# A transformer program on one core: new order in the ternary stage, three weight places in the expert stage, gathers ahead of a barrier

## The reference

```python
# block 0, feed-forward ("ffn0")
def act_quant(x):
    scale = 127.0 / jnp.clip(jnp.max(jnp.abs(x), axis=-1, keepdims=True), 1e-05)
    return jnp.clip(jnp.round(x * scale), -128, 127) / scale
h = bit_linear(x, w1)            # ternary weights, 256 -> 1024, input by act_quant
h = depthwise_conv1d(h.transpose(0, 2, 1), conv_w, conv_b)   # 3 taps over the positions
h = jax.nn.silu(h.transpose(0, 2, 1))
return bit_linear(h, w2)         # 1024 -> 256, input by act_quant

# block 1, feed-forward: 8 experts, 2 for each token ("moe"), then a layer norm ("norm2")
topv, topi = jax.lax.top_k(probs, K)
for e in range(E):
    h = jax.nn.relu(tok @ w1[e].T + b1[e]) @ w2[e].T + b2[e]
    moe_out = moe_out + combine[:, e:e + 1] * h
return _ln(x + moe_out, ln2_g, ln2_b)
```

## Time and profile before

| | us |
|---|---|
| median of 3 runs (lowest, highest) | 1503.93 (1497.29, 1506.65) |
| profiled execution, its own time | 1496.67 |
| its span, first to last instruction | 1495.1 |
| TensorE busy, share of the span | 76% |
| VectorE busy | 57% |
| GpSimd busy | 32% |
| ScalarE busy | 26% |
| TensorE's granted clock, mean (1 is 2.4 GHz, 0.5 is 1.2 GHz) | 0.856 |

### The profile page before, as it was taken

One profiled execution on the slowest core, in us unless ns is written; L12 is line 12 of the kernel. 1 busy time (PEld: TensorE's weight loads), 2 busy tenths in 40 slices (PEclk: granted clock), 3 DMA queues, 4 the chain that ended last, 5 costly groups with the idle time before them and its releaser, 6 DMA issues.

```text
span 1495.1 us, 20996 instructions
## 1 busy us (share of the span) xinstructions
PE 1141.2 (76%) x7256; PEld 951.7 (64%) x7257; DVE 855.3 (57%) x1924; ACT 381.6 (26%) x799; POOL 479.4 (32%) x351
## 2 busy tenths in 40 slices
PE   6889488884688696999469989999734998924574
PEld 4778376663577554898368878888623876612343
DVE  3676677855576547888512222222176785367985
ACT  1445122221455311111012212222211443201111
POOL 3434312234466023567640110000272332102210
PEclk9889699996799897999779999999865999555856
DMA  8998000000000200000341322110130000000000
GB/s 286 397 387 301 1 1 2 17 1 0 1 1 1 79 2 0 1 12 33 126 172 50 147 87 81 35 35 32 42 107 0 2 1 1 0 0 1 15 21 21
DMA packets 42860, 93.49 MB, mean 63 GB/s; under 512 B 3821, under 2 KB 16654, under 8 KB 39974
## 3 DMA queue, kind: packets, MB, share of 16 engines
q1 hardware_dynamic: 35254, 62.24, 11.5%
q0 software_dynamic: 7536, 30.32, 5.7%
HBM read 39.02 MB, written 51.51 MB: 61 GB/s over the span
## 4 chain that ended last, share of the span: by engine, by line
PE 60%; DVE 20%; issue 7%; POOL 5%; ACT 4%; DMA 3%; POOLq 1%; DVEq 0%; SPq 0%; ACTq 0%
PE PS L1864 9%; PE PS L1854 9%; PE PS L802 7%; PE PS L1131 3%; PE PS L785 3%; PE PS L815 3%; PE PS L1391 3%; PE PS L1731 3%; PE PS L775 2%; PE PS L757 2%; POOL big L1991 2%; PE PS L684 1%; PE PS L1720 1%; PE PS L2521 1%; PE PS L754 1%
## 5 line engine op out<-in xcount | busy, mean ns | idle before, releaser
L1854 PE MATMUL PS<-scr 128*128 128x128 f32 x1184 | 147.7, 285 | 14.1 <-DMA scr<-ew_in 9.6
L1854 PEld LDWEIGHTS PS<-scr 128*128 128x128 f32 x1184 | 146.1, 201 | 18.0 <-issue 13.4
L1864 PE MATMUL PS<-scr 128*128 128x256 f32 x592 | 136.6, 384 | 11.2 <-PE PS L1840 11.2
L1864 PEld LDWEIGHTS PS<-scr 128*128 128x128 f32 x592 | 109.6, 190 | 32.1 <-issue 18.9
L554 POOL TENSOR_TENSOR scr<-scr,big 128x1232 f32<-128x1232 f32 x32 | 72.0, 2249 | 142.5 <-DVE big L404 142.5
L1900 DVE TENSOR_SCALAR scr<-PS,W 128x128 f32<-128x128 f32 x148 | 51.5, 351 | 114.2 <-PE PS L1854 114.2
L1886 ACT ACTIVATE scr<-PS,W 128x128 f32<-128x128 f32 x148 | 54.3, 367 | 232.3 <-PE PS L1854 232.3
L1928 POOL DMA_DIRECT2D expert_out<-scr x37 | 20.1, 544 | 260.6 <-DVE scr L1906 260.6
L1906 DVE TENSOR_TENSOR scr<-PS,W 128x256 f32<-128x256 f32 x37 | 15.7, 425 | 146.0 <-PE PS L1864 146.0
L641 ACT ACTIVATE big<-PS 128x512 f32<-128x512 f32 x144 | 74.6, 525 | 96.1 <-PE PS L785 96.0
L785 PE MATMUL PS<-W,scr 128*128 128x128 f32 x480 | 82.8, 296 | 20.8 <-ACT scr L636 8.1
(11 more groups left out here) (382 smaller groups left out, 2364.6 us busy)
## 6 DMA issues: line engine op xcount, KB each, us to landing
expert_in<-zeros SPq DMA_DIRECT2D x1, 19712.0 KB, 60.0
expert_out<-zeros SPq DMA_DIRECT2D x1, 19712.0 KB, 111.9
scr<-ew_in POOLq DMA_DIRECT2D x16, 1024.0 KB, 6.2
scr<-expert_in SPq DMA_DIRECT2D x38, 128.0 KB, 2.0
expert_out<-scr POOLq DMA_DIRECT2D x37, 128.0 KB, 2.0
W<-pack SPq DMA_DIRECT2D x1, 2458.0 KB, 10.0
W<-pack SPq DMA_DIRECT2D x1, 2152.0 KB, 8.2
X<-x_in SPq DMA_DIRECT2D x1, 2048.0 KB, 12.8
```

The costliest lines, as they stand in the source:

```text
L1854: ins = pe.matmul(bank(1 + f % 4, G), e_w1[slot][:, k, f * P:(f + 1) * P], e_xT[:, k, :], start=(k == 0), stop=(k == C - 1))
L1864: ins = pe.matmul(bank(5 + t, D), e_h[:, f, t * P:(t + 1) * P], e_w2[slot][:, f, :], start=(f == 0), stop=(f == FC - 1))
```

## The change

**ffn0.** VectorE takes the statistics ahead of the scales instead of behind them. The maximum is taken apart: its first half stays behind the scales, then come rounding and the evacuation of the hidden products, and only then its second half, the join and the residual. TensorE transposes the maximum (`largest`) in the next turn, between the first two parts of the convolution, makes the output products of sample i-1 between the two halves of the hidden products, and the value or key products (`prepared`) at the end of a turn.

**moe.** The loop over pairs of experts is written out for all eight on every engine. A third weight place lies in `big`, so `slot` is e % 3, and GpSimd loads the weights of expert e + 3 once expert e is stored; those of experts 1 and 2 both at the start. TensorE no longer waits for its own transposes to tell SyncE that the rows' buffer is free; SyncE waits for their signal.

**norm2.** The gathers of samples 0 and 1 are issued at the end of moe, ahead of GpSimd's drain. The gathers are counted by six semaphores: one each for the samples 0, 1, 6 and 7, and one each for the pairs 2, 3 and 4, 5.

Elsewhere, a semaphore of the bias products becomes a count in an existing one, and two memsets share one.

```diff
@@ -943,12 +943,15 @@
                     v.tensor_tensor(f_G[:, 2 * p:2 * p + 2, 1:S + 1], bank(p % 2).rearrange("p (f s) -> p f s", f=2),
                                     f_row1.unsqueeze(1).broadcast_to([P, 2, S]), ALU.mult).then_inc(s["g_ready"], 1)
 
+            def largest_of(i, n):
+
+                v.wait_ge(s["silu_ready"], PAIRS * i + 2 * n + 2)
+                ch.inc(v.tensor_reduce(f_top[:, n, :], f_y[i % 2][:, n * PAIRS:(n + 1) * PAIRS, :].rearrange("p f s -> p s f"),
+                                       AX.X, ALU.max, apply_absolute_value=True))
+
             def largest(i):
 
-                for n in range(2):
-                    v.wait_ge(s["silu_ready"], PAIRS * i + 2 * n + 2)
-                    ch.inc(v.tensor_reduce(f_top[:, n, :], f_y[i % 2][:, n * PAIRS:(n + 1) * PAIRS, :].rearrange("p f s -> p s f"),
-                                           AX.X, ALU.max, apply_absolute_value=True))
+                largest_of(i, 1)
                 ch.sync()
                 v.tensor_tensor(f_amax, f_top[:, 0, :], f_top[:, 1, :], ALU.max).then_inc(s["amax_ready"], 1)
 
@@ -1001,16 +1004,18 @@
             for i in range(B):
                 if i + 1 < B:
                     quantized(i + 1)
+                if i + 2 < B:
+                    stats_of(i + 2)
                 if i:
                     scales(i - 1)
-                if i + 2 < B:
-                    stats_of(i + 2)
+                largest_of(i, 0)
+                if i:
+                    rounded(i - 1)
+                if i + 1 < B:
+                    hidden(i + 1)
                 largest(i)
                 if i:
-                    rounded(i - 1)
                     residual(i - 1)
-                if i + 1 < B:
-                    hidden(i + 1)
                 if i >= 5:
                     key_vars(v, ch, i - 5)
             scales(B - 1)
@@ -1177,6 +1182,8 @@
             pe.wait_ge(s["taps_ready"], FC)
             for i in range(B):
                 convolved(i, 0)
+                if i:
+                    largest(i - 1)
                 convolved(i, 1)
                 if i:
                     row2(i - 1)
@@ -1186,8 +1193,6 @@
                     normed(i + 1)
                     hidden(i + 1, 0)
                     hidden(i + 1, 1)
-                prepared(i)
-                largest(i)
                 if i:
                     if i == 1:
                         pe.wait_ge(s["w_ready"], 2)
@@ -1195,6 +1200,8 @@
                 if i + 1 < B:
                     hidden(i + 1, 2)
                     hidden(i + 1, 3)
+                prepared(i)
+            largest(B - 1)
             row2(B - 1)
             outputs(B - 1)
 
@@ -1250,8 +1257,9 @@
         TABLE_ROWS = -(-(MAX_GROUPS + AHEAD_MAX + 1) // 2) * 2 * G
         xg_dram = nc.dram_tensor("expert_in", (TABLE_ROWS, D), F32, kind="Internal").ap()
         yg_dram = nc.dram_tensor("expert_out", (TABLE_ROWS, D), F32, kind="Internal").ap()
-        e_w1 = [scr[:, n * 4096:n * 4096 + 2048].rearrange("p (c f) -> p c f", c=C) for n in range(2)]
-        e_w2 = [scr[:, n * 4096 + 2048:n * 4096 + 4096].rearrange("p (f d) -> p f d", f=FC) for n in range(2)]
+        e_slot = [scr[:, 0:4096], scr[:, 4096:8192], big[:, 2 * NT * D:2 * NT * D + 4096]]
+        e_w1 = [m[:, 0:2048].rearrange("p (c f) -> p c f", c=C) for m in e_slot]
+        e_w2 = [m[:, 2048:4096].rearrange("p (f d) -> p f d", f=FC) for m in e_slot]
         cut = Cut(scr, 8192)
         e_h = cut(FC * G).rearrange("p (f n) -> p f n", f=FC)
         e_x = scr[:, row8_at:row8_at + GT * D].rearrange("p (t d) -> p t d", t=GT)
@@ -1797,24 +1804,19 @@
 
         def moe_experts(eng, body, row_groups=False):
 
-            with eng.Fori(0, E // 2) as e2:
-                for slot in range(2):
-                    e = 2 * e2 + slot
-                    first = eng.value_load(GROUPS[0:1, bass.ds(e, 1)], min_val=0, max_val=MAX_GROUPS)
-                    last = eng.value_load(GROUPS[0:1, bass.ds(e + E, 1)], min_val=1, max_val=MAX_GROUPS)
-                    ahead = eng.value_load(GROUPS[0:1, bass.ds(e + 2 * E, 1)], min_val=0, max_val=AHEAD_MAX) if row_groups else None
-                    with eng.Fori(first, last) as n:
-                        body(n, slot, ahead if row_groups else e)
+            for e in range(E):
+                first = eng.value_load(GROUPS[0:1, e:e + 1], min_val=0, max_val=MAX_GROUPS)
+                last = eng.value_load(GROUPS[0:1, E + e:E + e + 1], min_val=1, max_val=MAX_GROUPS)
+                ahead = eng.value_load(GROUPS[0:1, 2 * E + e:2 * E + e + 1], min_val=0, max_val=AHEAD_MAX) if row_groups else None
+                with eng.Fori(first, last) as n:
+                    body(n, e % 3, ahead if row_groups else e)
 
         def rows_of(table, n):
             return table[bass.ds(n * G, G), :].rearrange("(t p) d -> p t d", p=P)
 
         def weights_load(eng, e, slot):
-            eng.dma_start(scr[:, slot * 4096:slot * 4096 + 2048], e_w(ew1_in, e)).then_inc(in_expert[slot], 16)
-            eng.dma_start(scr[:, slot * 4096 + 2048:slot * 4096 + 4096], e_w(ew2_in, e)).then_inc(in_expert[slot], 16)
-
-        def e_w(table, e):
-            return table[e] if isinstance(e, int) else table[bass.ds(e, 1), :, :].rearrange("e p n -> p (e n)")
+            eng.dma_start(e_slot[slot][:, 0:2048], ew1_in[e]).then_inc(in_expert[slot], 16)
+            eng.dma_start(e_slot[slot][:, 2048:4096], ew2_in[e]).then_inc(in_expert[slot], 16)
 
         def moe_sp(sp):
             sp.wait_ge(samp["slot_ready"], len(BATCHES) + 1)
@@ -1840,12 +1842,9 @@
                         ins = pe.transpose(bank(0, P, c * G + t * P), e_x[:, t, c * P:(c + 1) * P], ident)
                 ins.then_inc(s["xT_psum"], 1)
 
-                pe.wait_ge(s["xT_psum"], n + 1)
-                pe.sem_inc(s["x_free"], 1)
-
             def body(n, slot, e):
 
-                pe.wait_ge(in_expert[slot], 16 * (e - slot) + 32)
+                pe.wait_ge(in_expert[slot], 32 * (e // 3) + 32)
                 pe.wait_ge(s["xT_ready"], n + 1)
                 for f in range(FC):
 
@@ -1915,26 +1914,36 @@
             vb_zeroed(g, 2)
             g.wait_ge(in_rows, 16)
             weights_load(g, 1, 1)
+            weights_load(g, 2, 2)
             for n in range(2):
                 xs = X[:, n * B:(n + 1) * B, :]
                 g.tensor_tensor(xs, xs, w["ln2b"].unsqueeze(1).broadcast_to([P, B, D]), ALU.add)
 
-            def expert(e, slot):
-                first = g.value_load(GROUPS[0:1, bass.ds(e, 1)], min_val=0, max_val=MAX_GROUPS)
-                last = g.value_load(GROUPS[0:1, bass.ds(e + E, 1)], min_val=1, max_val=MAX_GROUPS)
-                ahead = g.value_load(GROUPS[0:1, bass.ds(e + 2 * E, 1)], min_val=0, max_val=AHEAD_MAX)
+            for e in range(E):
+                first = g.value_load(GROUPS[0:1, e:e + 1], min_val=0, max_val=MAX_GROUPS)
+                last = g.value_load(GROUPS[0:1, E + e:E + e + 1], min_val=1, max_val=MAX_GROUPS)
+                ahead = g.value_load(GROUPS[0:1, 2 * E + e:2 * E + e + 1], min_val=0, max_val=AHEAD_MAX)
                 with g.Fori(first, last) as n:
                     g.wait_ge(s["y_dve"], n + 2)
                     g.dma_start(rows_of(yg_dram, n + ahead), e_y).then_inc(rows_stored, 16)
                     g.wait_ge(rows_stored, 16 * n + 16)
                     g.sem_inc(s["y_sent"], 1)
-
-            with g.Fori(0, E // 2 - 1) as e2:
-                for slot in range(2):
-                    expert(2 * e2 + slot, slot)
-                    weights_load(g, 2 * e2 + slot + 2, slot)
-            for slot in range(2):
-                expert(E - 2 + slot, slot)
+                if e + 3 < E:
+                    weights_load(g, e + 3, e % 3)
+            gathered(g, 0)
+            gathered(g, 1)
+
+        ARRIVALS = [(0,), (1,), (2, 3), (4, 5), (6,), (7,)]
+
+        def arrival_of(i):
+            return [i in group for group in ARRIVALS].index(True)
+
+        def gathered(g, i):
+            for n in range(T * i, T * i + T):
+                for k in range(2):
+                    g.indirect_dma_start(got(k)[:, n, :], None, yg_dram,
+                                         bass.IndirectOffsetOnAxis(ap=SLOT[:, 2 * unit_of(n) + k:2 * unit_of(n) + k + 1], axis=0))\
+                        .then_inc(rows_gathered[arrival_of(i)], 16)
 
         def got(k):
             return e_got[k].rearrange("p (n d) -> p n d", n=NT)
@@ -1945,8 +1954,7 @@
             def summed(i):
 
                 y = n_y[i % 2]
-                if i % 2 == 0:
-                    v.wait_ge(rows_gathered[i // 2], 16 * 4 * T)
+                v.wait_ge(rows_gathered[arrival_of(i)], 16 * 2 * T * len(ARRIVALS[arrival_of(i)]))
                 for k in range(2):
                     for t in range(T):
                         n = T * i + t
@@ -1985,23 +1993,14 @@
         def norm2_pool(g):
             s = norm2
 
-            def gathered(i):
```

(10 more changed lines are left out.)

27 lines of the change are left out of this document (13 added, 14 removed).

## The result

The changed kernel takes 1465.88 us (median of 4 runs, 1462.73 to 1467.81) and the kernel before 1501.6 (4 runs, 1497.29 to 1506.65): a ratio of 0.9757, 95% interval 0.9726 to 0.9788. That is 35.7 us less; I had forecast 21.8 less, taken off a median of 1503.93, and the range ended at 1468. The profiled execution has a span of 1464.5 us, 30.6 less than before.

What follows compares the result with a forecast made beforehand. TensorE was taken to bound moe, a chain across engines ffn0, and GpSimd's queue norm2. Moe -25.9, norm2 -3.0 and ffn0 +7.1 gave -21.8 us off the 1503.93 median: 1482 us, range 1468 to 1494.

Steps and rivals of the forecast that it cites:

- TensorE's wait for its own transposes: In moe, removing this wait saves 0.28 us in each of 37 turns: -10.4 us, between -4 and -11.
- Expert weights: In moe, a third weight place removes two TensorE waits, 4.07 and 5.53 us, and slow products behind: -14.0 us.
- The change of expert: In moe, VectorE's late reading of the next expert's limits, charged 0.6 and 0.8 us where the weight waits go.
- rival C: In moe, the second expert's load delays the next groups' rows, costing 4 us: 1486 us; chance 0.08.
- Loops written out: In moe, dropping the outer expert loop saves 0.2 us at each of seven changes of expert: -1.5 us.
- rival D: In moe, repeated instruction loads cost 2.2 us a turn, making it slower, 1528 us with 21 such turns; chance 0.04.
- The loop of ffn0: The new order's turn takes 21.3 us against 20.44, +0.9, with TensorE waiting 2.8 us in one piece.
- each of four turns pays the lower clock: In ffn0, slow products behind TensorE's longer wait add 1.5 us a turn, from 0 to 3, over four turns.
- The tail: At the end of ffn0, earlier output products and last scales save 2.5 us, 0 to 4.
- the rival (A): TensorE keeps the higher clock in ffn0: 6 us less, 1476 us; chance 0.17.
- Norm2: Gathers ahead of the drain, about -1 us, and separate arrival signals, chiefly for sample 6: -3.0 us together.

Runs made afterwards that it cites:

- ffn_scales_first: The changed kernel with, on VectorE in ffn0, a sample's scales moved ahead of the next quantization and statistics; 1459.48 us, ratio 0.9705 to the kernel before.

## Why the prediction was wrong

- **TensorE's wait for its own transposes** is the step that failed. I wrote that it stood idle 0.30 us each time and took 0.28 x 37. The idle time is not the price of a wait: TensorE also lost the overlap of 0.16 and 0.07 in the products behind. 0.53 x 37 = 19.6 us against 10.4, more than the -11 that I gave as its bound. This alone, put in for my term, makes 1473, still inside the range; it takes the 6 us of ffn0 below as well to get to 1467, below its end. That TensorE's ends are modelled, as the Trainium skill says (Perfetto Trace Analysis, Tensor Engine Instruction (MATMUL, LD_WEIGHTS)), and the overlap with them, I could have seen: there too the groups that follow without a wait overlap by 0.16, and a turn's pieces, 3.69 + 3.73 + 0.38 + 0.30 = 8.10 us, make its 7.78 only with two such overlaps.
- **Expert weights**: right, and 1.4 us short. The turns of 14.93 and 16.32 us became 7.38 and 7.42. Less 0.53 each for the other term, that is 15.4 us against 14.0. The change of expert behind them costs 0.13 to 0.17, not 0.6 and 0.8, since the loops written out shorten it. The rows of the next groups were not delayed; rival C is out.
- **Loops written out**: 2.1 us at the five other changes against 1.5 for all; nothing of rival D.
- **The loop of ffn0** was right: 20.97 us for 21.3, the wait 2.84 for 2.8. Wrong was that each of four turns pays the lower clock. Two do, 1.68 us each, 3.4 in place of 6. The tail gave 3.7 us, not 2.5, and the stage +1.0 (+1.5 alone). I had the rival (A) and a price; what I lacked was a row on when a wait lowers the clock. The runs don't give a rule either: 2.84 us did it in two of four turns and 4.29 in each, but in ffn_scales_first 1.27 and 0.96 did it in three of five, and in the tail of before the slow products of the earlier trace rows come a wait of 1.59 us later.
- **Norm2**: -0.9 for -3.0. The early gathers bring nothing because the drain ends 4.9 us after the last of them, against 4.24 with none ahead: the two don't overlap. And the signals help from the last shared wait on, which is samples 4 and 5, not 6.
- **The rest.** The three stages that were changed make +1.0 - 38.1 - 0.9 = -38.0 us for the 35.7 of the medians, and att0 and att1 show that one stage alone can differ by 3 us and more between executions. The median that I took the sum off, 1503.93, lay 2.3 us above the 1501.6 of the result; this part of the miss in the time is luck of the runs.

## What to carry to other kernels

Price a wait by the distance from start to start of the work around it, not by the idle time beside its name; on TensorE it was 1.8 times the idle time in the middle of a loop's body (0.53 for 0.30 us), and 0.99 for 0.73 at its end. Where an order written by hand sets the turn, write down the loop through all engines and take out what needn't be in it: that was worth 28 us here, where the order that was tried gave nothing. Before a barrier with a drain, don't count a DMA that stands ahead of it as hidden.

## What the runs showed of the hardware

A wait at the end of a loop's body cost TensorE 0.99 us a turn, in its middle 0.53. Two VectorE instructions of 0.35 us took 2.44 and 2.43 when they met two of GpSimd's of 2.35 and 2.39 back to back: each waited for one. GpSimd's drain took 4.2 us with no gather ahead of it and ended 4.9 us after the last of eight; with the drain before it left out, the next one took 7.78 us in place of 2.93. The lowered clock came behind 2.84 us of waiting in two of four turns, in each of six traces, and behind 4.29 in each turn, and cost 24 convolution products 1.68 us each time, whatever the wait. It also came behind two waits of 1.27 and 0.96 us, in three turns of five.
